# Passage between two stages: one group's chain, two groups' turnings and some unread TensorE products in another order

## The chip, the cores and the metric

The kernel runs on one core of a Trainium2 chip. The core has five engines that run their own instruction lists side by side and wait for each other through semaphores: TensorE (PE), VectorE (DVE), ScalarE (ACT), GpSimd (POOL) and SyncE (SP, which only starts transfers here). The metric is the device time of one launch in microseconds, lower is better.

## The reference

The input `x` is 16 graphs of 512 nodes with 128 channels, `adj` 16 matrices of 512 x 512. The reference adds four blocks to `x`, each on a layer norm of it:

```
x = x + L0_gnn(layernorm(x), adj)      # normalized adjacency times a linear layer, relu
x = x + L0_ffn(layernorm(x))           # one linear layer
x = x + L1_gnn(layernorm(x), adj)      # two convolutions (the second of 17 taps), edge weights exp(-dist),
                                       # messages, a GRU-like update with gates r, z and candidate n
x = x + L1_ffn(layernorm(x))           # 30 steps of the recurrence below

def step(h):                           # h: 16 x 512 x 128
    h = h + 0.01 * tanh(h)
    h = h * sigmoid(h)                 # silu
    h = layernorm(h) * w + bias
    h = h @ W.T + b
```

## The kernel before

**Two stages.** The first stage walks over the 16 graphs; `step(b, p, c, d)` does the last part (gates and update) of graph `b` beside the first parts of the graphs after it. The second stage is the recurrence. Its 64 tiles of 128 tokens are cut into 8 groups of 8 tiles (128 x 1024 values each), and `slot(it, k)` is iteration `it` of group `k` on every engine. Groups depend on nothing but themselves, so all engines work on different groups at one time.

**One group's chain in one iteration.** ACT takes the tanh (`tanh`, L1026), DVE adds 0.01 of it (`scaled_sum`, L1360, tile `u_ring`), ACT takes the silu (`silu`, L1016, tile `g_pair`), DVE takes the statistics of it (`statistics`, L1343), POOL subtracts the mean (`centre`, L525, or `centre_one`, L531), the factor 1/sqrt of the variance comes from POOL (`power`, L516) for groups 0 to 3 of iteration 0 and from a chain of small DVE steps (`root_link`) elsewhere, POOL multiplies (`scale`, L543, tile `h_ring`), PE turns the eight tiles (L959), ACT copies them out (`state`, L1030), and PE multiplies them by the weights of the next iteration (`product_group`, L907) on top of a row of biases (`bias`, L924), which is written between the two halves of a turning.

**Semaphores.** `f_tanh`, `f_u`, `f_silu`, `f_bn`, `f_v`, `f_pow`, `f_norm`, `f_turn`, `f_state`, `f_mm` count these steps in the order of the groups: `f_norm` at 3 means that group 2 is scaled. `bias` for the product of group k waits until the sum of the group that used its banks before is done (`bias_free`, on `f_u`).

**The passage.** The last group (7) needs the last graph's update. In the last two steps of the first stage, `step(15, ...)` and `step(16, ...)` (marked `ends(b, B - 1)` and `ends(b, B)`), groups 0 to 6 of iteration 0 are therefore run in between the work on the last graph: the gates (`gates`, L1494 and L1498), the candidate (L1056), the update (`upd`, L1504, L1507, L1510), its turning on PE (L826), its addition to `x_tok` (L1543), its layer norm (`stats`, `rstd` on POOL, L505 and L507, `last_shift`, L1327, and `last_norm` on ACT, L1049), and then the tanh of group 7. The order of these pieces on every engine is written out by hand, and an engine never runs past a piece that waits. `keep_awake` (L637) issues products of the identity with itself that nobody reads.

**PSUM.** The turning of group j writes two of the banks 4 to 6 (`g_ps`), which the first stage uses as `CONV`, `CHAN` and `DIST_A`; its first half goes into the outer bank, the second into the one shared by even and odd groups.

## Time and profile before

| | us |
|---|---|
| median of 3 runs | 1262.13 (1261.93 to 1262.24) |
| the profiled execution | 1262.43 |
| its span in the trace | 1260.7 |
| PE busy | 1227.7 (97%) |
| DVE busy | 1151.1 (91%) |
| ACT busy | 961.3 (76%) |
| POOL busy | 950.1 (75%) |

The trace's times count from the start of the span. The first stage ends at about 542 us, the recurrence runs alone from about 560 us to the end. "Granted clock" is the share of its full speed that PE's clock was given: 1.00 is 2.4 GHz, 0.50 is 1.2 GHz. A bracket at a row's end is the time the engine sat idle before it and what ended that. Lengths of PE rows overlap, since products are pipelined: the distance from one start to the next is the better measure.

### The profile page before, as it was taken

The page shows a single profiled execution, that of the slowest core. Times are in us where ns is not written, and L with a number is a line of the kernel's source. Part 1 is how long each engine was busy: PE and PEld are TensorE (multiplying, and loading weights), DVE is VectorE, ACT ScalarE, POOL GpSimd, SP SyncE. Part 2 cuts the span into 40 slices and gives each one's busy share as a digit, 9 for nine tenths or more (in the row PEclk, how much of TensorE's full clock was granted, in tenths as well). Part 3 has the DMA queues.
Part 4 walks back from the last instruction along what each step waited for, and adds up shares of the span by engine and source line. Part 5 has one row for each costly group of instructions (what it writes and reads, how often), then busy time and mean ns, then how long its engine had stood idle before and what let it go on. Part 6 is the DMA issues. An engine that isn't in the chain of part 4 may idle for free.

```text
span 1260.7 us, 27945 instructions
## 1 busy us (share of the span) xinstructions
PE 1227.7 (97%) x9073; PEld 1094.8 (87%) x9073; DVE 1151.1 (91%) x3026; ACT 961.3 (76%) x1174; POOL 950.1 (75%) x668
## 2 busy tenths in 40 slices
PE   7899999999999999879999999999999999999998
PEld 6677777777777777669999999999999999999998
DVE  7988888888888887799999999999999999999996
ACT  2455555555555555779999999999999999999994
POOL 2455555555555555589999999999999999999996
PEclk9999999999999999979999999999999999999999
DMA  6111111111111100000000000000000000000004
GB/s 197 43 43 42 43 42 42 42 42 42 42 42 42 41 0 1 1 1 1 1 0 0 0 0 0 0 0 0 0 0 0 0 0 0 0 0 0 0 0 134
DMA packets 29814, 27.78 MB, mean 22 GB/s; under 512 B 3286, under 2 KB 21465, under 8 KB 29657
## 3 DMA queue, kind: packets, MB, share of 16 engines
q1 hardware_dynamic: 29784, 27.41, 6.9%
q8 instruction: 16, 0.26, 0.1%
q14 instruction: 14, 0.11, 0.0%
HBM read 23.21 MB, written 4.19 MB: 22 GB/s over the span
## 4 chain that ended last, share of the span: by engine, by line
PE 47%; DVE 3%; issue 2%; POOL 2%; ACT 1%; DVEq 0%; POOLq 0%
PE psum L907 28%; PE psum L959 15%; PE psum L924 3%; POOL h_ring L543 2%; DVE u_ring L1360 1%; ACT t_ring L1026 1%; DVE f_share L1397 1%; DVE f_stat L1343 1%; DVE psum L1402 0%; DVE psum L1413 0%; DVE psum L1416 0%; DVE f_rs L1431 0%; DVEq L389 0%; DVE y_all L1365 0%; DVEq L1341 0%
## 5 line engine op out<-in xcount | busy, mean ns | idle before, releaser
L543 POOL TENSOR_TENSOR h_ring<-g_pair,f_rs 128x1024 f32<-128x1024 f32 x240 | 452.4, 1906 | 31.2 <-DVE f_rs L1431 18.6
L1343 DVE BATCH_NORM_STATS2 f_stat<-g_pair 128x6 f32<-128x256 f32 x960 | 396.1, 427 | 2.4 <-ACT g_pair L1016 2.4
L959 PE MATMUL psum<-ident,h_ring 128*128 128x128 f32 (+1 forms) x1920 | 297.2, 277 | 4.1 <-POOL h_ring L543 3.1
L1360 DVE SCALAR_TENSOR_TENSOR u_ring<-t_ring,psum 128x1024 f32<-128x1024 f32 x232 | 282.3, 1217 | 5.7 <-issue 2.3
L959 PEld LDWEIGHTS psum<-ident,h_ring 128*128 128x128 f32 (+1 forms) x1920 | 248.1, 167 | 31.4 <-issue 3.7
L907 PE MATMUL psum<-w1c_t,y_all 128*128 128x128 f32 x1920 | 254.7, 276 | 0.0
L1030 ACT ACTIVATE y_all<-psum 128x1024 f32<-128x1024 f32 x240 | 243.9, 1016 | 14.1 <-PE psum L959 14.1
L907 PE MATMUL psum<-w_t,y_all 128*128 128x128 f32 x1920 | 254.5, 276 | 0.0
L1016 ACT ACTIVATE g_pair<-u_ring 128x1024 f32<-128x1024 f32 x240 | 251.7, 1049 | 0.0
L1026 ACT ACTIVATE t_ring<-psum 128x1024 f32<-128x1024 f32 x232 | 238.0, 1026 | 16.2 <-PE psum L907 9.6
L907 PEld LDWEIGHTS psum<-w1c_t,y_all 128*128 128x128 f32 x1920 | 234.6, 193 | 0.0
L907 PEld LDWEIGHTS psum<-w_t,y_all 128*128 128x128 f32 x1920 | 234.3, 192 | 0.0
L525 POOL TENSOR_TENSOR g_pair<-g_pair,f_stat 128x1024 f32<-128x1024 f32 x119 | 227.2, 1909 | 0.0
L505 POOL TENSOR_SCALAR ln_ve<-ln_stat 128x4 f32<-128x4 f32 x64 | 19.4, 302 | 130.7 <-DVE ln_stat L1289 130.7
L1012 ACT ACTIVATE work<-psum 128x512 f32<-128x512 f32 x64 | 34.8, 595 | 96.7 <-PE psum L774 96.6
L924 PE MATMUL psum<-bias,ones_bf 65*128 65x512 bf16 x240 | 92.0, 383 | 0.0
L692 PE MATMUL psum<-diff_s_h,wt_h 128*128 128x256 f32 x272 | 81.8, 301 | 0.0
L694 PE MATMUL psum<-diff_s_h,wt_l 128*128 128x256 f32 x272 | 77.0, 283 | 0.0
L693 PE MATMUL psum<-diff_s_l,wt_h 128*128 128x256 f32 x272 | 76.7, 282 | 0.0
L507 POOL TENSOR_TENSOR ln_rs<-ln_ve,half_neg 128x4 f32<-128x4 f32 x64 | 71.7, 1120 | 5.3
L511 POOL TENSOR_TENSOR work<-work 128x512 f32<-128x512 f32 x32 | 47.0, 1470 | 32.7 <-ACT work L1012 21.0
L1397 DVE TENSOR_REDUCE f_share<-psum 128x16 f32<-128x48 f32 x354 | 68.6, 194 | 0.1
(203 smaller groups left out, 2148.2 us busy)
## 6 DMA issues: line engine op xcount, KB each, us to landing
work<-in_adj_dram SPq DMA_DIRECT2D x16, 1024.0 KB, 5.5
x_tok<-in_x_dram SPq DMA_DIRECT2D x16, 256.0 KB, 5.6
out_dram<-y_all SPq DMA_DIRECT2D x7, 512.0 KB, 3.2
work<-in_L_gnn_conv_w_dram SPq DMA_DIRECT2D x1, 1088.0 KB
out_dram<-y_all SPq DMA_DIRECT2D x2, 256.0 KB, 3.6
work<-in_L_gnn_w_ih_dram SPq DMA_DIRECT2D x1, 384.0 KB
work<-in_L_gnn_w_hh_dram SPq DMA_DIRECT2D x1, 192.0 KB
work<-in_L_gnn_W_dram SPq DMA_DIRECT2D x1, 64.0 KB, 5.4
```

The costliest lines, as they stand in the source:

```text
L525: pool.tensor_tensor(two, two, means, ALU.subtract).then_inc(f_mean, 1)
L543: pool.tensor_tensor(tiles(h_ring[j % 4]), tiles(g_ring[j]), spread(f_rs[:, both(j), at:at + GT], GT, C), ALU.mult).then_inc(f_norm, 1)
L692: pe.matmul(dst, lhs[0], rhs[0], start=start, stop=False)
L907: m = pe.matmul(y_ps[k % 2][:, h, C * t:C * t + C], y_all[:, GT * k + NT * h + t, :], w1c_t[:] if h == centred(k) else w1_t[:], start=(h = ...
L924: pe.matmul(y_ps[k % 2][:, 1 - centred(k), :].rearrange("p (o n) -> p o n", o=2), ones_bf[:], four, start=True, stop=False, skip_group_che ...
L959: m = pe.transpose(g_ps[j % 2][0:rows, t // NT, P * (t % NT):P * (t % NT) + P], tiles(h_ring[j % 4])[:, t, 0:rows], ident[:])
L1016: act.activation(g_ring[j], u_ring[j % 2], ACT.Silu).then_inc(f_silu, 1)
L1026: act.activation(t_ring[k % 2], src, ACT.Tanh).then_inc(f_tanh, 1)
L1030: act.activation(y_all[:, GT * j:GT * j + GT, :].rearrange("p t c -> p (t c)"), g_ps[j % 2].rearrange("p h n -> p (h n)"), ACT.Copy).then_ ...
L1343: ins = dve.bn_stats(f_stat[:, j, 0, 2 * q:2 * q + 2, :].rearrange("p t w -> p (t w)"), two)
L1360: dve.scalar_tensor_tensor(out=u_ring[k % 2], in0=t_ring[k % 2], scalar=STEP, in1=src, op0=ALU.mult, op1=ALU.add).then_inc(f_u, 1)
L1397: dve.tensor_reduce(f_share[:], rows, AX_X, ALU.mult).then_inc(f_link, 1)
```

## The change

The chain of group 2 moves ahead: on ACT its silu stands ahead of the tanh of group 3, on DVE its statistics and variance ahead of the sum of group 3, and on POOL its scaling ahead of the last graph's `rstd`. The turnings of groups 0 and 1 move from the first two slots of PE's recurrence to a place ahead of the turning of the last update, with their copies on ACT (`state`) moved ahead as well. PE gets 12 unread products of 128 x 128 between the two turnings and 8 more (127 rows) ahead of the turning of group 3.

```diff
--- before.py
+++ after.py
@@ -592,10 +592,10 @@
                 if ends(b, B):
                     power(2)
                     centre_one(2)
+                    scale(0, 2, 2)
                 if later(b) and not ends(b, B - 1):
                     rstd(3, b - 1)
                 if ends(b, B):
-                    scale(0, 2, 2)
                     centre_one(3)
                     power(3)
                 if l1:
@@ -631,10 +631,10 @@
         @block.tensor
         def _(pe):
 
-            def keep_awake(bk, count):
+            def keep_awake(bk, count, rows=P):
 
                 for _ in range(count):
-                    pe.matmul(bank[bk][:, 0:P], ident[:], ident[:], start=True, stop=True)
+                    pe.matmul(bank[bk][0:rows, 0:P], ident[:, 0:rows], ident[:], start=True, stop=True)
 
             pe.wait_ge(s_ident, 1)
             keep_awake(DIST_B, 20)
@@ -723,6 +723,36 @@
                     m = pe.transpose(bk[:, P * t:P * t + P], adj_in[p][:, t, P * mt:P * mt + P], ident[:])
                 m.then_inc(s_adj_turned, 1)
 
+            def ones_row(b):
+
+                for t in range(0, NT, 2):
+                    pe.matmul(bank[b][:, C * t:C * t + 2 * C], ones_bf[:],
+                              bias1[:, 2:4, :].rearrange("p t c -> p (t c)"), start=(t == 0), stop=True,
+                              skip_group_check=True)
+
+            def turn_tile(j, n):
+                t = (n + NT * centred(j)) % GT
+                rows = P - 1 if n < NT else P
+                return pe.transpose(g_ps[j % 2][0:rows, t // NT, P * (t % NT):P * (t % NT) + P],
+                                    tiles(h_ring[j % 4])[:, t, 0:rows], ident[:])
+
+            def first_turn(j):
+
+                if j == 0:
+                    pe.wait_ge(s_conv_pre, B)
+                    ones_row(CONV)
+                else:
+                    pe.wait_ge(s_r, B)
+                    ones_row(DIST_A)
+                pe.wait_ge(f_norm, j + 1)
+                for n in range(GT):
+                    if n == NT and j == 0:
+                        pe.wait_ge(s_x_nmp_lo, B)
+                    elif n == NT:
+                        pe.wait_ge(f_state, 1)
+                    m = turn_tile(j, n)
+                m.then_inc(f_turn, 1)
+
             def step(b, p, c, d):
                 q = 1 - p
                 l1 = exists(b)
@@ -819,6 +849,11 @@
 
                     if l1:
                         pe.wait_ge(s_common_read, b + 1)
+                    if ends(b, B):
+                        first_turn(0)
+                        pe.wait_ge(s_msg_pre, B)
+                        keep_awake(TOK, 12)
+                        first_turn(1)
                     pe.wait_ge(s_upd, b)
                     if not l1:
                         pe.wait_ge(s_x3, b - 1)
@@ -924,13 +959,6 @@
                 pe.matmul(y_ps[k % 2][:, 1 - centred(k), :].rearrange("p (o n) -> p o n", o=2), ones_bf[:], four,
                           start=True, stop=False, skip_group_check=True)
 
-            def ones_row(b):
-
-                for t in range(0, NT, 2):
-                    pe.matmul(bank[b][:, C * t:C * t + 2 * C], ones_bf[:],
-                              bias1[:, 2:4, :].rearrange("p t c -> p (t c)"), start=(t == 0), stop=True,
-                              skip_group_check=True)
-
             def slot(it, k):
                 if not ends(it, 0):
                     product_group(it, k)
@@ -938,33 +966,24 @@
                 ahead = not (ends(it, 0) and k < GROUPS - 1) and not (ends(it, ITERS) and k == GROUPS - 1)
                 if before is not None:
                     i, j, s = before
-                    if ends(i, 0) and j == 0:
-                        pe.wait_ge(s_conv_pre, B)
-                        ones_row(CONV)
-                    elif ends(i, 0) and j == 1:
-                        pe.wait_ge(s_r, B)
-                        ones_row(DIST_A)
-                    else:
-                        pe.wait_ge(f_state, s - 1)
+                    pe.wait_ge(f_state, s - 1)
+                    if ends(i, 0) and j == 3:
+                        keep_awake(CHAN + 1, 8, P - 1)
                     pe.wait_ge(f_norm, s + 1)
                 for n in range(GT):
                     if before is not None:
                         if n == NT:
-                            if ends(i, 0) and j == 0:
-                                pe.wait_ge(s_x_nmp_lo, B)
-                            else:
-                                pe.wait_ge(f_state, s)
-                        t = (n + NT * centred(j)) % GT
-                        rows = P - 1 if n < NT else P
-                        m = pe.transpose(g_ps[j % 2][0:rows, t // NT, P * (t % NT):P * (t % NT) + P],
-                                         tiles(h_ring[j % 4])[:, t, 0:rows], ident[:])
+                            pe.wait_ge(f_state, s)
+                        m = turn_tile(j, n)
                     if ahead and n == NT - 1:
                         bias_free(it, k)
                         bias((k + 1) % GROUPS)
                 if before is not None:
                     m.then_inc(f_turn, 1)
 
-            slots(pe, slot, LAG_T, 2)
+            bias_free(0, GROUPS - 1)
+            bias(0)
+            slots(pe, slot, GROUPS, 2)
 
 
 
@@ -1086,13 +1105,13 @@
                     wait(act, s_ffn, c)
                     act.activation(xh_t[:], bank[TURN_B], ACT.Copy).then_inc(s_xt[0], 1)
                 if ends(b, B):
+                    state(0, 0)
                     tanh(0, 4)
                     silu(3, 3)
                     tanh(0, 5)
-                    state(0, 0)
+                    state(1, 1)
                     silu(4, 4)
                     tanh(0, 6)
-                    state(1, 1)
                     silu(5, 5)
                     last_norm()
                 if l1:
@@ -1135,6 +1154,7 @@
                     act.wait_ge(s_nmp, b + 1)
                     act.activation(x_nmp[0][:], bank[CHAN], ACT.Copy).then_inc(s_x_nmp, 1)
                 if ends(b, B - 1):
+                    silu(2, 2)
                     tanh(0, 3)
                 if d is not None:
                     adjt_even(d, p, 2)
@@ -1146,8 +1166,6 @@
                 if ends(b, B - 2):
                     tanh(0, 0)
                     tanh(0, 1)
-                if ends(b, B - 1):
-                    silu(2, 2)
                 if l0:
 
                     act.wait_ge(s_turn[2], c + 1)
@@ -1510,7 +1528,6 @@
                     dve.scalar_tensor_tensor(out=upd[:], in0=upd[:], scalar=0.5, in1=n_act[:],
                                              op0=ALU.mult, op1=ALU.add).then_inc(s_upd, 1)
                 if ends(b, B):
-                    variance(2)
                     scaled_sum(0, 4)
                 if l1:
 
@@ -1605,8 +1622,9 @@
                 if ends(b, B - 1):
                     variance(0)
                     variance(1)
+                    statistics(2, 2)
+                    variance(2)
                     scaled_sum(0, 3)
-                    statistics(2, 2)
                 if l0:
 
                     dve.wait_ge(s_xt[2], c + 1)
```

ACT in the passage, before. `g_pair<-u_ring` is a silu, `t_ring<-y_all` a tanh, `y_all<-psum` a `state`, the three `gates` are gh_n, r and z, `n_act` the candidate.

```order
L1026 ACTIVATE t_ring<-y_all 128x1024
L1145 ACTIVATE gates<-psum,bcol 128x512
L1016 ACT_TABLE_LOAD
L1016 ACTIVATE g_pair<-u_ring 128x1024
L1163 ACTIVATE gates<-psum,bcol 128x512
L1167 ACTIVATE gates<-psum,bcol 128x512
L1056 ACTIVATE n_act<-gates,bcol 128x512
L1026 ACTIVATE t_ring<-y_all 128x1024
L1016 ACTIVATE g_pair<-u_ring 128x1024
L1026 ACTIVATE t_ring<-y_all 128x1024
L1030 ACTIVATE y_all<-psum 128x1024
L1016 ACTIVATE g_pair<-u_ring 128x1024
```

And after the change:

```order
L1035 ACT_TABLE_LOAD
L1035 ACTIVATE g_pair<-u_ring 128x1024
L1045 ACTIVATE t_ring<-y_all 128x1024
L1165 ACTIVATE gates<-psum,bcol 128x512
L1181 ACTIVATE gates<-psum,bcol 128x512
L1185 ACTIVATE gates<-psum,bcol 128x512
L1075 ACTIVATE n_act<-gates,bcol 128x512
L1049 ACTIVATE y_all<-psum 128x1024
L1045 ACTIVATE t_ring<-y_all 128x1024
L1035 ACTIVATE g_pair<-u_ring 128x1024
L1045 ACTIVATE t_ring<-y_all 128x1024
L1049 ACTIVATE y_all<-psum 128x1024
```

The table load and the silu of group 2 have moved ahead of a tanh and gh_n; the first `state` has moved ahead of two tanhs and a silu, the second ahead of the silu of group 4.

POOL in the same place, before. `f_rs` is `power`, L531 `centre_one`, `ln_ve` and `ln_rs` the last graph's `rstd`, `h_ring` `scale`.

```order
L516 TENSOR_TENSOR f_rs<-f_var,half_neg 128x8
L531 TENSOR_TENSOR g_pair<-g_pair,f_stat 128x512
L505 TENSOR_SCALAR ln_ve<-ln_stat 128x4
L507 TENSOR_TENSOR ln_rs<-ln_ve,half_neg 128x4
L543 TENSOR_TENSOR h_ring<-g_pair,f_rs 128x1024
L531 TENSOR_TENSOR g_pair<-g_pair,f_stat 128x512
L516 TENSOR_TENSOR f_rs<-f_var,half_neg 128x8
L543 TENSOR_TENSOR h_ring<-g_pair,f_rs 128x1024
```

After:

```order
L516 TENSOR_TENSOR f_rs<-f_var,half_neg 128x8
L531 TENSOR_TENSOR g_pair<-g_pair,f_stat 128x512
L543 TENSOR_TENSOR h_ring<-g_pair,f_rs 128x1024
L505 TENSOR_SCALAR ln_ve<-ln_stat 128x4
L507 TENSOR_TENSOR ln_rs<-ln_ve,half_neg 128x4
L531 TENSOR_TENSOR g_pair<-g_pair,f_stat 128x512
L516 TENSOR_TENSOR f_rs<-f_var,half_neg 128x8
L543 TENSOR_TENSOR h_ring<-g_pair,f_rs 128x1024
```

The scaling of group 2 has moved ahead of `rstd`; everything else keeps its place.

PE, before, from the last product of the first stage on. `bias` in a row is the row of biases (two of 256 are written ahead of the first turnings).

```order
L694 MATMUL psum<-x_nmp_h,wt_l 128x512
L826 MATMUL psum<-ident,upd 128x128 x4
L930 MATMUL psum<-bias,ones_bf 128x256 x2
L959 MATMUL psum<-ident,h_ring 127x128 x4
L959 MATMUL psum<-ident,h_ring 128x128 x4
L930 MATMUL psum<-bias,ones_bf 128x256 x2
L959 MATMUL psum<-ident,h_ring 127x128 x4
L924 MATMUL psum<-bias,ones_bf 128x512
L959 MATMUL psum<-ident,h_ring 128x128 x4
L907 MATMUL psum<-w1c_t,y_all 128x128 x4
L907 MATMUL psum<-w_t,y_all 128x128 x4
L959 MATMUL psum<-ident,h_ring 127x128 x4
```

After:

```order
L694 MATMUL psum<-x_nmp_h,wt_l 128x512
L729 MATMUL psum<-bias,ones_bf 128x256 x2
L736 MATMUL psum<-ident,h_ring 127x128 x4
L736 MATMUL psum<-ident,h_ring 128x128 x4
L637 MATMUL psum<-ident 128x128 x12
L729 MATMUL psum<-bias,ones_bf 128x256 x2
L736 MATMUL psum<-ident,h_ring 127x128 x4
L736 MATMUL psum<-ident,h_ring 128x128 x4
L861 MATMUL psum<-ident,upd 128x128 x4
L959 MATMUL psum<-bias,ones_bf 128x512
L942 MATMUL psum<-w1c_t,y_all 128x128 x4
L942 MATMUL psum<-w_t,y_all 128x128 x4
```

The turnings of groups 0 and 1 and 12 unread products now stand ahead of the turning of `upd`, which was the first of them. The bias row of group 0's product (128x512), which lay inside the second turning, now stands behind it. Eight more unread products follow further down, between the product of group 1 and the turning of group 3.

On DVE the diff tells it all: the statistics and the variance of group 2 stand ahead of the sum of group 3, which itself stands ahead of everything of `step(16, ...)`.

## Rows read from the trace of the kernel before

**Rows 1.** Part 1 of the page: busy time of each engine.

```profile
PE 1227.7 (97%) x9073; PEld 1094.8 (87%) x9073; DVE 1151.1 (91%) x3026; ACT 961.3 (76%) x1174; POOL 950.1 (75%) x668
```

**Rows 2.** Stretches of the span; columns: from:to, length, busy per engine, granted clock.

```profile
536.00:538.00 2.00, 0.00 (x0) 0.00 (x0) 1.97 (x6) 0.84 (x2) 1.94 (x1) 0.93 0.00 0
546.00:548.00 2.00, 2.00 (x10) 1.70 (x10) 2.00 (x5) 2.00 (x4) 2.00 (x2) 0.51 0.00 0
554.00:556.00 2.00, 0.33 (x1) 0.36 (x2) 2.00 (x9) 2.00 (x3) 2.00 (x2) 0.70 0.00 0
560.00:562.00 2.00, 2.00 (x13) 1.99 (x12) 1.38 (x7) 0.27 (x1) 2.00 (x2) 0.59 0.04 8
560.00:1200.00 640.00, 639.03 (x5446) 614.39 (x5446) 634.43 (x1960) 625.05 (x653) 611.13 (x327) 1.00 0.00 0
```

**Rows 3.** PE in order of time, the passage; columns: start, length, instruction, idle before.

```profile
541.83 1.11 PE L826 MATMUL psum<-ident,upd 128*128 128x128 f32 x4 [6.80 <-DVE upd L1510]
...
550.58 1.06 PE L907 MATMUL psum<-w_t,y_all 128*128 128x128 f32 x8
551.47 1.06 PE L907 MATMUL psum<-w1c_t,y_all 128*128 128x128 f32 x8
555.67 1.19 PE L959 MATMUL psum<-ident,h_ring 128*127 128x128 f32 x4 [3.15 <-POOL h_ring L543]
...
557.22 1.06 PE L959 MATMUL psum<-ident,h_ring 128*128 128x128 f32 x4
558.07 1.91 PE L907 MATMUL psum<-w1c_t,y_all 128*128 128x128 f32 x8
...
562.66 1.06 PE L907 MATMUL psum<-w_t,y_all 128*128 128x128 f32 x8
```

**Rows 4.** ACT in order of time, same stretch and columns.

```profile
529.30 1.05 ACT L1026 ACTIVATE t_ring<-y_all 128x1024 f32<-128x1024 f32 x1
...
531.59 1.28 ACT L1016 ACT_TABLE_LOAD   x1
...
549.79 1.64 ACT L1049 ACTIVATE y_all<-x_tok,ln_shift,ln_rs 128x128 f32<-128x128 f32 x4
...
555.22 1.01 ACT L1030 ACTIVATE y_all<-psum 128x1024 f32<-128x1024 f32 x1
```

**Rows 5.** DVE in order of time, same stretch and columns.

```profile
538.79 2.27 DVE L1507 SCALAR_TENSOR_TENSOR upd<-gates,upd 128x512 f32<-128x512 f32 x1
541.09 0.69 DVE L1510 SCALAR_TENSOR_TENSOR upd<-upd,n_act 128x512 f32<-128x512 f32 x1
...
542.99 0.69 DVE L1543 TENSOR_TENSOR x_tok<-x_tok,psum 128x512 f32<-128x512 f32 x1
...
548.52 0.51 DVE L1327 SCALAR_TENSOR_TENSOR ln_shift<-ln_stat,ln_rs 128x4 f32<-128x4 f32 x1
...
555.55 1.21 DVE L1360 SCALAR_TENSOR_TENSOR u_ring<-t_ring,psum 128x1024 f32<-128x1024 f32 x1
```

**Rows 6.** POOL in order of time, same stretch and columns.

```profile
531.90 1.92 POOL L525 TENSOR_TENSOR g_pair<-g_pair,f_stat 128x1024 f32<-128x1024 f32 x1
533.96 1.90 POOL L543 TENSOR_TENSOR h_ring<-g_pair,f_rs 128x1024 f32<-128x1024 f32 x1
...
538.01 2.49 POOL L543 TENSOR_TENSOR h_ring<-g_pair,f_rs 128x1024 f32<-128x1024 f32 x1
541.94 2.55 POOL L516 TENSOR_TENSOR f_rs<-f_var,half_neg 128x8 f32<-128x8 f32 x1 [1.44 <-DVE f_var L1384]
544.47 1.04 POOL L531 TENSOR_TENSOR g_pair<-g_pair,f_stat 128x512 f32<-128x512 f32 x1
...
546.73 2.28 POOL L543 TENSOR_TENSOR h_ring<-g_pair,f_rs 128x1024 f32<-128x1024 f32 x1
...
551.03 1.64 POOL L516 TENSOR_TENSOR f_rs<-f_var,half_neg 128x8 f32<-128x8 f32 x1
552.75 2.78 POOL L543 TENSOR_TENSOR h_ring<-g_pair,f_rs 128x1024 f32<-128x1024 f32 x1
```

## Prediction

> **What bounds the kernel now.** First the page: PE is busy 97% of the span, DVE 91% [rows 1]. The stretches then say where this share comes from: from 560 us on PE is busy 639.03 of 640 us at full clock [rows 2]. From its re-entry on, the recurrence is PE's own work and nothing is waited for long. The diff touches nothing inside that loop, so the change can only shift the moment at which PE enters it for good. All that follows is read between 528 and 563 us.
>
> PE in order of time shows this passage [rows 3]. After the last gate product it is idle 6.80 us, from 535.0, until DVE's update lets it turn `upd` at 541.83. It works until about 552.4 us, is idle 3.15 us and starts again at 555.67 with the turning of group 3, because `h_ring` of that group is late. From there on no gap follows. The granted clock goes with the idle time [rows 2]: 536 to 538 has a mean of 0.93, so it fell to 1.2 GHz at about 537.7, and it was back at 2.4 GHz by 548.1 (the stretch up to 548 is still 0.51). The second stretch at 1.2 GHz begins at about 554.8 (mean 0.70 from 554 to 556) and ends at about 561.6 (0.59 from 560 to 562). So there is idle time, twice, and half speed, twice; only what delays the entry counts. Between 555.67 and 561.6 PE works at half speed, which costs (561.6 - 555.67) / 2 = 3.0 us.
>
> Two chains end at this entry. On POOL: eight large operations of which each follows the one before it. The first part of the turning of group 3 needs the last of them, the scaling that begins at 552.75 and takes 2.78 [rows 6]. On ACT: `last_norm` begins at 549.79, then come four large operations and the `state` of group 2 at 555.22, which ends at 556.23 [rows 4]. PE's next product of group 2, at 558.07, needs that `state`. Between the halves of the turning stands a bias row, and it waits for the sum of group 0's iteration 1, which DVE ends at 555.55 + 1.21 = 556.76 [rows 5]; the second half starts at 557.22. That sum comes out of the same ACT chain. So even a `h_ring` of group 3 that is there at 553 lets PE do only four turnings; then it stands again until some 7.0 us after `last_norm` begins (556.76 - 549.79).
>
> **The change, part by part.**
>
> ACT: the table load and silu 2 ahead of tanh 3. Both now stand where tanh 3 started, at 529.30 [rows 4]. Load 1.28, silu 1.05 as the tanh: the silu ends at about 531.7 instead of 531.59 + 2.33 = 533.9, 2.2 us earlier. Nothing is added, there is one load as before. Tanh 3 ends at 532.7 instead of 530.35; gh_n follows it, still ahead of gate r.
>
> DVE: statistics and variance of group 2 run 531.8 to 533.2, ahead of the sum of group 3. That sum, which had run beside POOL's `power`, now meets POOL's centring of group 0 (531.90 + 1.92 = 533.82) and scaling of group 0 (from 533.96) [rows 6]. The row that prices this is `upd` at 538.79: 2.27 us against 0.69 for the same kind of operation at 541.09 [rows 5]; it ended 0.56 after POOL's scaling (538.01 + 2.49 = 540.50), as if it had only begun when POOL was through. The Trainium skill ("SBUF — State Buffer", Who interferes with whom) says that a DVE instruction with two SBUF inputs and a GpSimd instruction that reads SBUF exclude each other for a whole instruction; this row agrees. So I lay them one behind the other: sum 3 at 533.8 to 534.9, the scaling of group 0 from 534.9 to 536.8 (before: 535.86), 0.9 us late; if DVE's next gate operation gets in ahead too, 1.5 us late. Bounds: 0 to 1.6. I take 0.9 to 1.5.
>
> POOL after that: `power` 1 and the scaling of group 1 keep their work and end at about 541.2 (between 540.9 and 541.5; before 540.50). Now comes the gain. `power` 2 had waited 1.44 us for its variance and then took 2.55 [rows 6]; the variance has long been there. It runs 1.64, as the row at 551.03, until about 543.2, 544.2 at worst, `centre_one` 1.04 more [rows 6], and the scaling of group 2, ahead of `rstd`, ends at 546.2 to 547.1. Before it ended at 546.73 + 2.28 = 549.01, so 2 to 3 us are won for group 2. PE has no use for them that counts: the turning of group 2 was over at 550.6 and PE idle from 552.4. The last graph's `rstd` pays: it stands behind a scaling of 1.9 us and ends at 547.9 to 549.3 instead of ahead of 546.73, where the scaling began. Then `centre_one`, `power` 3 and the scaling of group 3: 1.04 + 1.64 + 1.9 = 4.6 us and up to 2 us of waiting for DVE's sums, so `h_ring` of group 3 at 552.9 to 555.6 instead of 555.53.
>
> PE: turnings 0 and 1 and the unread products ahead of `upd`. Turning 0 needs `h_ring` 0, at 536.8 to 537.4, and takes 0.9 at full speed. Each unread product is two passes; eight passes take 551.47 - 550.58 = 0.89 us at full speed [rows 3], so 24 take 2.7, and 5.3 at half speed. They run beside the wait for `h_ring` 1 (541.2): at full speed they are hidden and end at 541.1. But PE was idle from 535.0 to 536.8 here and the clock fell at 537.7 before; if it falls again they end at 542.8 or so. Turning 1 then ends at 542.1 or 543.9, and only behind it stands the turning of `upd`, which itself is ready at 539.5 to 543.0. `upd` is turned by 542.9 to 544.4 (before 542.9), and its addition to `x_tok` starts at 543.1 to 544.5 (before 542.99 [rows 5]). On ACT the two early `state` copies cost 1.0 each, as the one at 555.22; what hides them is that ACT, with all before silu 5 done by 547, waits for DVE's sum of group 5 in any case.
>
> What the addition decides: behind it DVE has statistics 0.9, the statistics of group 3 1.4, the sum of group 5 1.2, the statistics of group 4 1.4 and `last_shift`, together 5.6 us from its start: 548.6 before, plus a wait (`last_shift` took 0.51 us from 548.52 [rows 5]). `last_norm` could thus have begun at 549.0 (548.52 + 0.51); it began at 549.79, since ACT was still busy. ACT is free earlier now, so this bound falls away, and DVE's takes its place: 543.1 to 544.5 plus 5.6 plus up to 0.8 of waiting for POOL gives 548.7 to 550.9. The middle is 550.0, 0.2 us later than before. The second half of turning 3 starts at 550.0 + 7.4 = 557.4 instead of 557.22, and group 2's product at 558.3.
>
> The 8 unread products ahead of turning 3: 1.8 us at full speed behind the product of group 1, which ends at 550.2 to 552. They end at 552 to 553.8 and are hidden, as PE waits until 557.4 in any case, but for four turnings. From 553.8 at the latest, and 554.4 with those, 3 us or more of nearly nothing remain; a gap of 3.15 us lowered the clock before. So I expect the second stretch at 1.2 GHz again, with the same end near 561.6 and the same cost.
>
> Sum: profiled execution 1262.43 + 0.2 = 1262.6. The median of the runs is 0.30 below the profiled one, so 1262.3 us. My forecast for itself spans 1261.6 to 1263.3.
>
> **Rivals.** Times are for the median. A difference of under 0.2% (2.5 us) is what a measurement of this kernel can't tell from none.
>
> A. The clock stays up. If the unread products and the four early turnings of group 3 keep it at 2.4 GHz, PE does the work from 557.2 on at full speed: 0.4 for the second half, 1.8 for the product, 559.5. Then it needs `h_ring` 4, which POOL can't end before 559.3 to 559.7, and 1.1 for turning it: 560.6 instead of 562.66 [rows 3], 2.1 us won. With `last_norm` at 549.0 it is 2.8. For it: the first idle stretch of 6.8 us is filled. Against it: the wait in front of the bias is not filled. 1260.0, a chance of 0.2.
>
> B. The queue in front of `upd` (the side of slower). Mechanism: the clock falls at 537.7, the 24 passes run at half speed, turning 1 and `upd` come late, `x_tok` at 545.1 instead of 542.99. It decides once the addition starts after 544.2; each 1 us from there is 1 us at the entry: 0.9 us. PE then enters so late, or with a stop in front of the bias, that the clock comes back later: the first stretch at 1.2 GHz lasted 10.4 us against 6.8 of the second [rows 2], half of the difference is 1.8. Together 2.7: 1264.8. The late `upd` alone has a chance of 0.3 and is worth under 1; with the clock 0.13.
>
> C. The change does not do what it says: `h_ring` 2 not earlier, because DVE's sums take the place of POOL's old wait. Then `rstd`, behind a scaling that ends at 549.01 as before, would end at 550.3 (1.3 us more, as from 545.5 to the scaling's start at 546.73), `last_norm` would begin at 550.8, 1.0 late, and the time would be 1263.1. The chance is 0.1.
>
> **How the numbers follow.** Forecast (0 to +1 around) 0.57, A 0.2, B with the clock 0.13, C 0.1. Of A about two thirds reach 2.5 us, of B nearly all, of C and the forecast nearly nothing: faster by over 0.2% 0.13, slower 0.13, within it 0.74. The range from 1260.1 to 1264.5 leaves out half of A and most of B, less than 0.2.
>
> **What would show it.** In the profile after: silu 2 ending near 531.7; no idle time of POOL near 541; `h_ring` 2 at 546.2 to 547.1 and `h_ring` 3 by 555.6; PE rows of `upd` at 542.5 to 544; `last_norm` between 549 and 551; PE's second half of turning 3 some 7.4 us behind it; clock at half from 555 to 561.6. I am wrong if PE stays at 2.4 GHz through 555 to 561, if `last_norm` moves by over 1 us, or if the stretch from 563 us to the end changes its length.

## The result and the profile after

The changed kernel takes 1264.28 us (median of 22 runs, 1263.07 to 1265.48) against 1261.91 us (22 runs, 1260.85 to 1262.96) of the kernel before: ratio 1.0018, 95% interval 1.0012 to 1.0024. It is 2.4 us slower, 0.18%. The time was forecast at 1262.3 in a range of 1260.1 to 1264.5; the side was right, the size of the loss was not.

The profiled execution has a span of 1262.8 us. The loop did not change: from the product of group 3 (562.66 before [rows 3], 564.74 after) to the last product row of each trace (1254.92 and 1256.98) they take 692.3 and 692.2 us. Of the 2.1 us between the two traces, 0.24 are there at the sum of group 2 (527.74 before, 527.98 after), before the first moved instruction, and fall to no part of the change: the trace after has a short stretch at 1.2 GHz near its start (0.93 from 10 to 15 us, 0.73 from 15 to 20) that the trace before lacks. The other 1.8 us arise in the passage.

The profile after, PE in order of time (start, length, instruction, idle time before it). L736 is a turning, L637 the unread products, L861 the turning of `upd`, L959 the bias row, L942 a product.

```profile
536.94 1.14 PE L736 MATMUL psum<-ident,h_ring 128*127 128x128 f32 x8 [1.44 <-POOL h_ring L543]
537.92 2.84 PE L637 MATMUL psum<-ident 128*128 128x128 f32 x24
...
542.87 0.66 PE L861 MATMUL psum<-ident,upd 128*128 128x128 f32 x4
...
554.71 0.71 PE L736 MATMUL psum<-ident,h_ring 128*127 128x128 f32 x4 [2.78 <-POOL h_ring L543]
558.78 0.61 PE L959 MATMUL psum<-bias,ones_bf 65*128 65x512 bf16 x1 [3.36 <-DVE u_ring L1378]
559.18 1.06 PE L736 MATMUL psum<-ident,h_ring 128*128 128x128 f32 x4
...
564.74 1.06 PE L942 MATMUL psum<-w_t,y_all 128*128 128x128 f32 x8
```

These answer to [rows 3]. The first idle stretch (6.80 us) is filled but for waits of 1.44, 0.61 and 1.08 us, and the clock stayed up through it. The first half of turning 3 comes at 554.71, counted from the sum of group 2 (the start of the passage) 1.2 us earlier than before. But then PE stands 3.36 us ahead of the bias row, which had followed at once before, and the second half comes at 559.18 instead of 557.22.

ACT, DVE and POOL after, in three parts, the same columns. L1068 is `last_norm`, L1345 `last_shift`, L1378 the sums, L543 the scalings, L507 the end of `rstd`, L516 `power`.

```profile
530.96 1.06 ACT L1035 ACTIVATE g_pair<-u_ring 128x1024 f32<-128x1024 f32 x1
...
550.08 1.65 ACT L1068 ACTIVATE y_all<-x_tok,ln_shift,ln_rs 128x128 f32<-128x128 f32 x4 [0.84 <-DVE ln_shift L1345]
...
555.77 1.06 ACT L1035 ACTIVATE g_pair<-u_ring 128x1024 f32<-128x1024 f32 x1 [1.10 <-DVE u_ring L1378]
```

```profile
535.05 2.38 DVE L1512 SCALAR_TENSOR_TENSOR gates<-gates 128x512 f32<-128x512 f32 x1
...
543.87 0.68 DVE L1560 TENSOR_TENSOR x_tok<-x_tok,psum 128x512 f32<-128x512 f32 x1
...
549.42 0.63 DVE L1345 SCALAR_TENSOR_TENSOR ln_shift<-ln_stat,ln_rs 128x4 f32<-128x4 f32 x1
...
552.85 2.89 DVE L1378 SCALAR_TENSOR_TENSOR u_ring<-t_ring,y_all 128x1024 f32<-128x1024 f32 x1 [0.33 <-ACT t_ring L1045]
...
557.52 1.20 DVE L1378 SCALAR_TENSOR_TENSOR u_ring<-t_ring,psum 128x1024 f32<-128x1024 f32 x1
```

```profile
534.20 2.69 POOL L543 TENSOR_TENSOR h_ring<-g_pair,f_rs 128x1024 f32<-128x1024 f32 x1
...
541.50 2.09 POOL L516 TENSOR_TENSOR f_rs<-f_var,half_neg 128x8 f32<-128x8 f32 x1
...
545.00 1.90 POOL L543 TENSOR_TENSOR h_ring<-g_pair,f_rs 128x1024 f32<-128x1024 f32 x1
...
547.14 1.87 POOL L507 TENSOR_TENSOR ln_rs<-ln_ve,half_neg 128x4 f32<-128x4 f32 x1
548.99 1.04 POOL L531 TENSOR_TENSOR g_pair<-g_pair,f_stat 128x512 f32<-128x512 f32 x1
549.99 2.69 POOL L516 TENSOR_TENSOR f_rs<-f_var,half_neg 128x8 f32<-128x8 f32 x1
552.76 1.90 POOL L543 TENSOR_TENSOR h_ring<-g_pair,f_rs 128x1024 f32<-128x1024 f32 x1
```

The row to look for is DVE's at 552.85: the sum of group 7 takes 2.89 us. Before, it began at 552.55 and took 1.23:

```profile
552.55 1.23 DVE L1360 SCALAR_TENSOR_TENSOR u_ring<-t_ring,y_all 128x1024 f32<-128x1024 f32 x1 [1.04 <-ACT t_ring L1026]
```

POOL's scaling of group 3, from 552.75, took 2.78 [rows 6] instead of 1.90. The sum begins 0.09 us behind POOL where it had been 0.20 us ahead. Which of the two moved is read from the start of the passage, the sum of group 2, since the whole passage lies 0.24 us later in this trace. Counted from there the sum of group 7 comes 0.06 us later (24.81 and 24.87), with `last_norm` (22.05 and 22.10), and POOL's scaling comes 0.23 us earlier (25.01 and 24.78). So the order turned mainly because POOL was early. DVE now waits for POOL where POOL had waited for DVE. POOL's 0.9 us had cost nothing; DVE's 1.7 us lie on the chain to the bias row, and ACT's silu of group 7 waits for it too (1.10 us idle).

The granted clock after, in stretches (from:to, length, busy times, clock):

```profile
538.00:540.00 2.00, 2.00 (x20) 2.00 (x20) 1.97 (x7) 1.81 (x3) 1.92 (x2) 1.00 0.00 0
556.00:558.00 2.00, 0.00 (x0) 0.00 (x0) 2.00 (x9) 2.00 (x3) 1.51 (x1) 0.75 0.00 0
562.00:564.00 2.00, 2.00 (x12) 2.00 (x12) 1.34 (x7) 0.31 (x1) 2.00 (x2) 0.54 0.00 0
```

In the passage there is one stretch at 1.2 GHz left, from about 557 to 563.8, and it lies over PE's re-entry as the second one did before [rows 2].

### The profile page after: what moved, and what is told of

It reads as the page before. It is cut to its first block, busy times and chain, and to the rows that moved or that the text cites. A ratio compares the mean times of both kernels' runs of the same rounds, so it can differ in the third digit from the quotient of the medians.

```text
span 1262.8 us, 28024 instructions
## 1 busy us (share of the span) xinstructions
PE 1232.4 (98%) x9113; PEld 1098.6 (87%) x9113; DVE 1153.8 (91%) x3026; ACT 961.7 (76%) x1174; POOL 951.3 (75%) x668
## 4 chain that ended last, share of the span: by engine, by line
PE 77%; DVE 11%; issue 4%; ACT 3%; POOL 2%; DVEq 0%; DMA 0%; SPq 0%; POOLq 0%; ACTq 0%
PE psum L942 28%; PE psum L736 15%; PE psum L692 5%; PE psum L694 5%; PE psum L693 5%; PE psum L898 4%; PE psum L959 3%; PE psum L714 3%; PE psum L709 3%; POOL h_ring L543 2%; DVE u_ring L1378 1%; PE psum L723 1%; PE psum L703 1%; DVE emb_n L1556 1%; ACT t_ring L1045 1%
## 5 line engine op out<-in xcount | busy, mean ns | idle before, releaser
L543 POOL TENSOR_TENSOR h_ring<-g_pair,f_rs 128x1024 f32<-128x1024 f32 x240 | 451.9, 1904 | 33.2 <-DVE f_rs L1449 20.6
L736 PE MATMUL psum<-ident,h_ring 128*128 128x128 f32 (+1 forms) x1920 | 295.2, 276 | 6.1 <-POOL h_ring L543 5.1
L1378 DVE SCALAR_TENSOR_TENSOR u_ring<-t_ring,psum 128x1024 f32<-128x1024 f32 x232 | 281.7, 1214 | 6.0 <-issue 2.3
L736 PEld LDWEIGHTS psum<-ident,h_ring 128*128 128x128 f32 (+1 forms) x1920 | 246.0, 166 | 33.8 <-POOL h_ring L543 9.0
L942 PE MATMUL psum<-w_t,y_all 128*128 128x128 f32 x1920 | 254.5, 276 | 0.0
L942 PE MATMUL psum<-w1c_t,y_all 128*128 128x128 f32 x1920 | 254.5, 276 | 0.0
L942 PEld LDWEIGHTS psum<-w_t,y_all 128*128 128x128 f32 x1920 | 234.3, 192 | 0.0
L942 PEld LDWEIGHTS psum<-w1c_t,y_all 128*128 128x128 f32 x1920 | 234.3, 192 | 0.0
L959 PE MATMUL psum<-bias,ones_bf 65*128 65x512 bf16 x240 | 91.8, 382 | 4.4 <-DVE u_ring L1378 3.4
L507 POOL TENSOR_TENSOR ln_rs<-ln_ve,half_neg 128x4 f32<-128x4 f32 x64 | 72.5, 1133 | 5.3
```

Of the source, the lines that this page charges most:

```text
L543: pool.tensor_tensor(tiles(h_ring[j % 4]), tiles(g_ring[j]), spread(f_rs[:, both(j), at:at + GT], GT, C), ALU.mult).then_inc(f_norm, 1)
L736: return pe.transpose(g_ps[j % 2][0:rows, t // NT, P * (t % NT):P * (t % NT) + P], tiles(h_ring[j % 4])[:, t, 0:rows], ident[:])
L942: m = pe.matmul(y_ps[k % 2][:, h, C * t:C * t + C], y_all[:, GT * k + NT * h + t, :], w1c_t[:] if h == centred(k) else w1_t[:], start=(h = ...
L1378: dve.scalar_tensor_tensor(out=u_ring[k % 2], in0=t_ring[k % 2], scalar=STEP, in1=src, op0=ALU.mult, op1=ALU.add).then_inc(f_u, 1)
```

## The experiments

Each was timed beside the kernel before on the same chip (11 runs each, e2 7). The expectations weigh three explanations of the loss. "Port order" is my theory: a sum of DVE and an operation of POOL exclude each other, the one that begins first goes on and the other waits for its end, and at the sum of group 7 this order has turned. "Queue in front of upd" is rival B of the prediction, and "clock" is a half-speed stretch that ends later for reasons of its own.

The sum of group 2 is the last large instruction ahead of all that was moved, and it starts between 527.02 and 528.14 us in the ten traces; so distances are compared, not times. Five of them carry the readings: from the sum of group 2 to `last_norm` (a), from `last_norm` to the sum of group 0 in iteration 1 that frees the bias row (b), the length of the sum of group 7, from the sum of group 2 to the bias row of turning 3 (bias), and from there to the first product of group 3 (c), behind which PE is in the loop. The sum of the last two says when PE enters it: 34.92 us before, 36.76 after the change.

| kernel | median us | ratio to before (95% interval) | a | b | sum 7 | bias | c |
|---|---|---|---|---|---|---|---|
| before | 1261.9 | 1 | 22.05 | 5.76 | 1.23 | 29.08 | 5.84 |
| changed | 1264.28 | 1.0018 (1.0012 to 1.0024) | 22.10 | 7.44 | 2.89 | 30.80 | 5.96 |
| e1_hold | 1261.55 | 0.9997 (0.9988 to 1.0006) | 22.09 | 5.77 | 1.22 | 29.16 | 4.78 |
| e2_before_late | 1266.04 | 1.0032 (1.0020 to 1.0043) | 22.06 | 9.58 | 2.81 | 32.91 | 6.03 |
| e3_turns_only | 1259.87 | 0.9985 (0.9976 to 0.9994) | 21.26 | 5.77 | 1.23 | 29.19 | 3.55 |
| e4_chain_only | 1263.49 | 1.0015 (1.0006 to 1.0024) | 22.84 | 6.85 | 2.30 | 30.95 | 4.91 |
| e5_no_unread | 1262.52 | 1.0006 (0.9997 to 1.0015) | 22.30 | 5.91 | 1.35 | 29.47 | 5.72 |
| e6_hold_28 | 1260.76 | 0.9992 (0.9983 to 1.0001) | 22.10 | 5.79 | 1.23 | 29.16 | 4.22 |
| e7_turns_filled | 1259.74 | 0.9983 (0.9974 to 0.9992) | 21.27 | 5.79 | 1.23 | 28.70 | 3.82 |
| e8_pool_undone | 1260.73 | 0.9991 (0.9982 to 1.0000) | 21.96 | 5.78 | 1.23 | 29.01 | 4.20 |

The columns split what happens at the entry. The change loses 1.72 us up to the bias row and 0.12 behind it. The kernels that are faster than before (e3, e6, e7, e8) write the bias row at nearly the same distance as before, 28.70 to 29.19 us against 29.08; what they win lies nearly all behind it, in c, where PE turns and multiplies at 2.4 GHz instead of 1.2.

**e1_hold**, the changed kernel with the meeting of the two taken away:

```diff
 def scale(i, j, s):
     ...
+    if ends(i, 0) and j == 3:
+        pool.wait_ge(f_u, 8)
     at = GT * (j % 2)
```

> The changed kernel, and POOL waits ahead of the scaling of group 3 until DVE's sum of group 7 is done (f_u at 8); nothing else differs. Port order (my theory): in the changed kernel that sum took 2.89 us instead of 1.2, since POOL's scaling of group 3 began 0.09 us before it. With the wait the sum takes 1.2 us, the scaling starts near 554.0 and h_ring of group 3 comes at 556, which is still ahead of the bias row; the bias row of turning 3 comes at 557.1 instead of 558.78, and the time falls by 1.7 us to 1262.6. Queue in front of upd (rival): the loss comes from x_tok, late by 0.6 us, and all behind it; the wait changes nothing there and the scaling comes 1.3 us later: 1264.3 or up to 1.3 more. Clock (rival): the second stretch at 1.2 GHz ended at 563.6 instead of 561.6 of itself; the time stays at 1264.3.

Measured: 1261.55 us, 2.7 less than the changed kernel. The sum takes 1.22 us again, POOL idles 1.56 us, its scaling comes 1.5 us later (26.26 behind the sum of group 2 instead of 24.78), and b is back at 5.77. The first two blocks are DVE and POOL of this kernel, the third PE.

```profile
552.05 1.22 DVE L1380 SCALAR_TENSOR_TENSOR u_ring<-t_ring,y_all 128x1024 f32<-128x1024 f32 x1 [0.33 <-ACT t_ring L1047]
```

```profile
549.19 2.69 POOL L516 TENSOR_TENSOR f_rs<-f_var,half_neg 128x8 f32<-128x8 f32 x1
553.45 1.90 POOL L545 TENSOR_TENSOR h_ring<-g_pair,f_rs 128x1024 f32<-128x1024 f32 x1 [1.56 <-DVE u_ring L1380]
```

```profile
555.40 1.16 PE L738 MATMUL psum<-ident,h_ring 128*127 128x128 f32 x4 [4.26 <-POOL h_ring L545]
556.35 0.63 PE L961 MATMUL psum<-bias,ones_bf 65*128 65x512 bf16 x1
556.78 1.06 PE L738 MATMUL psum<-ident,h_ring 128*128 128x128 f32 x4
...
561.13 1.06 PE L944 MATMUL psum<-w_t,y_all 128*128 128x128 f32 x8
```

A wait more makes the changed kernel faster. This is the port order's outcome and neither rival's. It is 1.0 us more than the 1.7 that the sum explains. The traces say where the two parts lie: the bias row comes 1.64 us earlier, as expected, and 1.18 us more are won behind it (c 4.78 instead of 5.96), since the half-speed stretch was short here (clock 0.87 from 554 to 556, 0.50 from 556 to 558 and 0.77 from 558 to 560). The other runs agree: the mean granted clock of all 11 is 0.9975, that of the changed kernel's 22 is 0.9958.

**e2_before_late**, the kernel before with the order of the changed one forced on it:

```diff
 def scaled_sum(it, k):
     ...
     wait(dve, f_silu, s - 1)
+    if ends(it, 0) and k == 7:
+        dve.wait_ge(f_norm, 4)
```

> The kernel before, and DVE waits ahead of the sum of group 7 until POOL has scaled group 3 (f_norm at 4): the order that the changed kernel falls into, forced on the old one. Port order: POOL's scaling runs 552.75 to 554.65 (1.9 instead of 2.78), the sum ends at 555.9 instead of 553.78, the bias row of turning 3 comes 2.1 us later, and the time rises by 2.1 us to 1264.0. Queue in front of upd: this kernel has no such queue, and h_ring of group 3 comes 0.9 us earlier: 1261.9 or less. Clock: 1261.9.

Measured: 1266.04 us, 4.2 more than before, with nothing of the change in it but the order of two instructions, which a wait forces. That is twice what I had expected. DVE and POOL of this kernel show why:

```profile
554.56 2.81 DVE L1362 SCALAR_TENSOR_TENSOR u_ring<-t_ring,y_all 128x1024 f32<-128x1024 f32 x1 [3.26 <-POOL h_ring L543]
```

```profile
552.53 1.90 POOL L543 TENSOR_TENSOR h_ring<-g_pair,f_rs 128x1024 f32<-128x1024 f32 x1
554.38 1.91 POOL L525 TENSOR_TENSOR g_pair<-g_pair,f_stat 128x1024 f32<-128x1024 f32 x1
```

The sum, let go when the scaling ends, meets POOL's next instruction at once and waits for that one as well: b grows by 3.8 us. So e2 shows the direction and more than the size of what the changed kernel lost, where the sum waited for one instruction only. The scaling of group 3 takes 1.90 us here, and `h_ring` comes earlier than in the kernel before, which is of no use.

**e3_turns_only** leaves of the change only the early turnings of groups 0 and 1, their `state` copies and the unread products:

```diff
 # POOL, step(16): scale(0, 2, 2) behind rstd(3, ...) again
 # ACT, step(15): silu(2, 2) behind tanh(0, 3) and gh_n again
 # DVE: scaled_sum(0, 3) ahead of statistics(2, 2); variance(2) behind the update again
```

> The changed kernel with group 2's chain put back on ACT, DVE and POOL; only the early turnings with their copies and the unread products are left of the change. Port order: POOL and DVE meet as in the kernel before, the sum of group 7 comes first; ACT is free for last_norm, which starts 0.7 us earlier, at 549.1: 1261.2. Queue in front of upd: the turning of upd comes behind 24 passes and a turning, x_tok at 543.5 to 544 instead of 542.99: 1262.4 to 1264.3.

Measured: 1259.87 us, 2.0 less than before, 4.4 less than the change. `last_norm` comes 0.8 us earlier (a), as expected, and x_tok's addition is not late: it starts 15.17 us behind the sum of group 2, and 15.25 before. The sum of group 7 begins 0.91 us ahead of POOL's scaling and is clear of it. The early turnings with the unread products are thus a gain, and the queue in front of `upd` is no cost here.

The gain does not come by way of the earlier `last_norm`, though. PE of this kernel:

```profile
552.97 1.82 PE L942 MATMUL psum<-w1c_t,y_all 128*128 128x128 f32 x8
554.63 1.94 PE L637 MATMUL psum<-ident 128*127 128x128 f32 x16
556.40 0.61 PE L736 MATMUL psum<-ident,h_ring 128*127 128x128 f32 x4
556.84 0.38 PE L959 MATMUL psum<-bias,ones_bf 65*128 65x512 bf16 x1
...
560.39 1.06 PE L942 MATMUL psum<-w_t,y_all 128*128 128x128 f32 x8
```

The sum that frees the bias row ended at 555.90, but PE was still at its own work, the first part of it at 1.2 GHz, and wrote the row 29.19 us behind the sum of group 2, 0.1 us later than before. What is won is c, 3.55 us instead of 5.84: the half-speed stretch lay ahead of the re-entry (clock 0.50 from 548 to 554) and not over it.

**e4_chain_only** is the other half: the kernel before with the moves of group 2's chain on POOL, ACT and DVE, and PE's order left.

> The kernel before with only group 2's chain moved ahead on ACT, DVE and POOL; PE's order and the state copies stay. Port order: upd is late by 1.0 us (DVE and POOL exclude each other around 534 to 537), ACT's chain with it, so last_norm starts at 550.8; the scaling of group 3 starts ahead of the sum of group 7, which loses another 1 us or so: 1263.9. Queue in front of upd: there is none here, and the time is 1261.9 to 1262.9.

Measured: 1263.49 us, 1.6 more than before. `last_norm` is 0.8 us later, the sum of group 7 begins 0.68 us behind POOL's scaling and takes 2.30. Both losses are of the expected kind and size; the bias row comes 1.87 us later, and in this trace 0.93 of that come back in c. DVE's row, then POOL's:

```profile
552.62 2.30 DVE L1359 SCALAR_TENSOR_TENSOR u_ring<-t_ring,y_all 128x1024 f32<-128x1024 f32 x1 [0.91 <-ACT t_ring L1026]
```

```profile
551.94 1.90 POOL L543 TENSOR_TENSOR h_ring<-g_pair,f_rs 128x1024 f32<-128x1024 f32 x1
```

**e5_no_unread** drops both `keep_awake` calls from the changed kernel.

> The changed kernel without its 12 and 8 unread products. Port order (my theory): they run beside waits and lie on no path; upd, x_tok, last_norm and the sum of group 7 come at the same times, and turning 3 is already at half speed with them: 1264.3, at most 1 us more where the clock falls more often. Queue in front of upd (rival): 24 passes leave the queue ahead of the turning of upd, x_tok comes earlier by up to 0.6 us: 1263.7 or less.

Measured: 1262.52 us, 1.8 less. Neither expectation holds. x_tok's addition came not earlier but later (16.59 us behind the sum of group 2, 15.89 in the changed kernel), for the clock fell: 0.50 from 542 to 544. By this delay the sum of group 5 came at 19.66 us behind the sum of group 2 instead of 18.95, while the last graph's `rstd` began at 19.2 in both. So `rstd` ran in 1.01 us ahead of that sum, where in the changed kernel it took 1.87 us behind it. POOL's `power` 3 began 0.46 us ahead of the sum of group 6 and took 1.64 instead of 2.69, and the scaling of group 3 began 1.62 us ahead of the sum of group 7, which lost only 0.1 us by it (1.35):

```profile
546.33 1.01 POOL L507 TENSOR_TENSOR ln_rs<-ln_ve,half_neg 128x4 f32<-128x4 f32 x1
547.30 1.63 POOL L531 TENSOR_TENSOR g_pair<-g_pair,f_stat 128x512 f32<-128x512 f32 x1
548.89 1.64 POOL L516 TENSOR_TENSOR f_rs<-f_var,half_neg 128x8 f32<-128x8 f32 x1
550.61 1.90 POOL L543 TENSOR_TENSOR h_ring<-g_pair,f_rs 128x1024 f32<-128x1024 f32 x1
```

So in these two traces the unread products cost nothing by lying in the queue; they placed DVE and POOL so that they met, and without them the bias row comes 1.33 us earlier. The theory held, but I had taken the meeting for granted instead of working out whether it would still take place.

**e8_pool_undone** puts back one line, POOL's scaling of group 2 behind `rstd`; PE, ACT and DVE are those of the changed kernel.

> The changed kernel with only POOL's order put back: rstd of the last graph ahead of the scaling of group 2 again. rstd ends near 546.9 instead of 549.0, last_norm comes at 549.6 instead of 550.1, the tanh of group 7 ends at 552.3, POOL's scaling of group 3 starts at about 552 to 553.5. Port order: the time depends on which of the two comes first; if the sum does, it takes 1.2 us and the bias row comes at 556.5: 1262.0; if not, 1263.8. Queue in front of upd: that queue is unchanged and x_tok as late as in the changed kernel: 1264.3.

Measured: 1260.73 us, 3.5 less than the changed kernel and 1.1 less than before. The sum comes first (551.79, 1.23 us) and POOL's scaling behind it (552.70, 2.07). This line alone decides about the loss: without it the rest of the change is at the edge of a gain (the interval ends at 1.0000). I had expected 1262.0 for this case with the bias row at 556.5 on the changed kernel's clock. It came at 556.07 in a trace that runs 0.92 us ahead of that one, so 0.5 us later than expected. The time was lower than expected all the same, because PE was at full speed by then: c is 4.20 us instead of 5.96, which is half of the 3.5 us. The bias row gives the other half (29.01 instead of 30.80).

**e6_hold_28 and e7_turns_filled** ask for the clock's share. The first is e1 with 28 unread products instead of 8, the second e3 with

```diff
                 pe.wait_ge(f_state, s - 1)
+                if ends(i, 0) and j == 2:
+                    keep_awake(CONV, 14, P - 1)
                 if ends(i, 0) and j == 3:
-                    keep_awake(CHAN + 1, 8, P - 1)
+                    keep_awake(CHAN + 1, 18, P - 1)
```

> The changed kernel with the wait of the first experiment (sum of group 7 first) and 28 unread products ahead of turning 3 in place of 8. The 8 ended at 551.1 there and PE stood 4.3 us; 28 take 6.2 us and end at 555.4, as h_ring of group 3 comes. If the half clock at the entry still costs time, PE now turns and multiplies at full speed from 555.4 on, until h_ring of group 4 (559.2) bounds it: 0.8 us less than without, 1260.8. If the entry is bounded by the bias row and h_ring of group 4 alone, 1261.5. If the 28 products run at half speed themselves they end at 561 and the time is over 1264.

> The third experiment (early turnings only, group 2's chain as before the change) with 14 unread products ahead of turning 2 and 18 instead of 8 ahead of turning 3. There the clock fell at 548.3, PE having stood 3.3 us ahead of turning 2, and product and turnings up to 555.1 ran at half speed. Filled, it stays at 2.4 GHz; the bias row of turning 3 comes right behind the sum at 555.9 instead of 556.84, the next product at 556.8 instead of 557.5; h_ring of group 4 at 558.8 then bounds PE: 0.5 us less, 1259.4. If the clock is no part of it: 1259.9. If the added products come in the way of turning 2 (h_ring at 548.9): up to 1 us more.

Measured: 1260.76 us, 0.8 less than e1, as expected. PE of e6 stays at full clock (1.00 in every stretch from 540 to 562), and the wait goes to `h_ring` of group 4:

```profile
549.08 6.37 PE L639 MATMUL psum<-ident 128*127 128x128 f32 x56
555.28 0.69 PE L738 MATMUL psum<-ident,h_ring 128*127 128x128 f32 x4
556.21 0.39 PE L961 MATMUL psum<-bias,ones_bf 65*128 65x512 bf16 x1 [0.23 <-DVE u_ring L1380]
...
559.26 0.68 PE L738 MATMUL psum<-ident,h_ring 128*127 128x128 f32 x4 [0.44 <-POOL h_ring L545]
```

The 0.8 us are what the clock still cost in e1, whose half-speed stretch was short. Against the kernel before, with the bias row at the same distance, c is 4.22 us instead of 5.84.

e7 took 1259.74 us against 1259.87 of e3: no difference that these runs can tell, where 0.5 was expected. The bias row comes 0.49 us earlier in its trace, as expected, but 0.27 of that go again in c. In e3's trace the half-speed stretch lay ahead of the re-entry (from about 547.8 to 554.5, and not from 548.3 to 555.1 as my expectation has it), where it costs little. e7 is the fastest kernel of the study, 2.1 us (0.17%, interval 0.08 to 0.26%) under the kernel before and 4.5 under the change; e3, which differs from it by nothing measurable, has the simpler code.

## Why the prediction was right and wrong

**Right: what bounds the passage.** `last_norm` at 550.08 was forecast at 550.0; counted from the sum of group 2 it is 0.05 us later than before, where 0.2 was forecast. Behind it the bias row, not `h_ring` of group 3, lets PE in: `h_ring` came at 554.66, 0.9 us earlier than before on the trace's clock, and bought nothing, as in e2. The loop kept its length. One reading of [rows 6] was loose: of POOL's large operations not each follows the one before it, as `power` 2 had waited 1.44 us for its variance.

**Right: the steps on ACT, DVE and POOL up to 549 us.** Silu 2 ended at 532.0 (531.7 forecast). The scaling of group 0 ended at 536.89 (536.8), DVE's gate operation waited for it (2.38 us), POOL had no idle time near 541, `h_ring` of group 2 ended at 546.90 (546.2 to 547.1), the last graph's `rstd` at 549.01 (547.9 to 549.3). x_tok's addition came at 543.87 (543.1 to 544.5).

**Wrong: "PE's second half of turning 3 some 7.4 us behind" `last_norm`.** It came 9.1 us behind. This is the term that was mis-sized, and it holds nearly all of the 1.8 us that arose in the passage: b grew by 1.68 us. I took the stretch from `last_norm` to the bias row as a constant, since none of its instructions was moved. I had used the exclusion of DVE's and POOL's instructions elsewhere, and for this place too, but only one way round: "up to 2 us of waiting for DVE's sums", POOL's wait. [rows 6] showed a scaling of 2.78 us, which says that the sum had got in just ahead of it; the trace has it at 552.55, 0.20 us ahead. My own forecast moved both against this margin, `last_norm` by 0.2 us and POOL's scaling by up to 2.6 (its end at 552.9 to 555.6 instead of 555.53). e1 and e2 show the cause from both sides: the order of these two instructions, put right in the changed kernel, gives back 2.7 us, of which 1.64 lie ahead of the bias row, and put wrong in the old one it costs 4.2, with a second instruction to wait for.

**What turned the margin** is shown by e8 to be the order on POOL. With `rstd` first, the sum of group 7 comes 0.14 us earlier and POOL's scaling 0.86 us later (25.64 behind the sum of group 2 instead of 24.78), because POOL's scaling of group 2 and centring of group 3 each wait for one of DVE's sums there (2.98 and 2.09 us, in the changed kernel 1.90 and 1.04). Group 2's chain on ACT and DVE makes `last_norm` 0.7 us later (e8 against e3: 21.96 and 21.26) and the time 0.9 (1260.73 and 1259.87, with intervals of the ratios that overlap).

**Rival A, the clock stays up:** half of it took place. The first half-speed stretch is gone from the profile; `last_norm` came no earlier by it, and what it was worth was not isolated. The second stayed, as forecast: PE had stood 2.78 us ahead of turning 3 and stood 3.36 more ahead of the bias row. It is no part of the loss (c 5.84 and 5.96). Its price is large all the same, and the faster kernels live on it: c is 1.6 us shorter than before in e6 and e8, 2.0 in e7 and 2.3 in e3. The 2.1 that I gave it had the right size, and so had the bound by `h_ring` of group 4: PE gets it in e6 at 559.26, which is 559.95 on the clock of the kernel before, where 559.3 to 559.7 was forecast.

**Rival B, the queue in front of `upd`:** wrong as a mechanism. The clock did not fall at 537.7, the 24 passes took 2.84 us, and e3 has the same queue and is the second fastest. The addition to `x_tok` is 0.6 us late in the changed kernel and 0.8 in e4, which has no such queue, and not late in e3, which has it; in e8, where only POOL's order is put back, it is 0.6 late. So the delay comes with group 2's chain on ACT and DVE. The rival's price of 2.7 us came near the measured loss by chance. **Rival C** did not happen: `h_ring` 2 was early.

**Open:** why the clock came back sooner in e1 than in the changed kernel, which is worth the 1.0 us of e1's 2.7 that the sum does not explain, and what decides in general where the half-speed stretch falls. e3 and e8 gained by its place without being built for it. Open too is the difference between the 2.4 us of the medians and the 1.8 that the passage shows in the two traces, as only one execution of each kernel was traced.

## What to carry to other kernels

Where two engines exclude each other on an instruction, look at each such pair near the critical chain and write down which comes first and by how much; a margin of 0.2 us between two instructions of 1.2 and 1.9 us is a term of the sum, even if nothing there is edited. If the order matters, fix it with a wait, as in e1: the engine with slack should be the one that waits. Then split the time at the entry into the part up to the wait that ends last and the part behind it: here the order of two instructions moved the first, and the place of PE's half-speed stretch moved the second by as much, so that a kernel can win for another reason than the one it was written for (e3). And an operation moved ahead pays only if its result is what somebody waits for; here the early scaling of group 2 gave a result that PE had no use for, and by sparing POOL two waits it brought POOL's next scaling ahead of the sum on which the end hung.

## What the runs showed of the hardware that was not expected

An instruction that loses once can lose twice: in e2 the sum was ready at the moment when POOL's scaling ended, POOL's centring began 0.18 us ahead of it, and the sum took 2.81 us. POOL's `power`, an operation of 1.64 us on few values, can lose too: it took 2.69 when one of DVE's sums had begun 0.02 us ahead of it (549.97 and 549.99 in the changed kernel). The other way round neither lost. In the kernel before, `power` began first, and the sum of group 3 ran beside it in its usual length; DVE's row, then POOL's:

```profile
530.39 1.23 DVE L1360 SCALAR_TENSOR_TENSOR u_ring<-t_ring,y_all 128x1024 f32<-128x1024 f32 x1
```

```profile
530.29 1.64 POOL L516 TENSOR_TENSOR f_rs<-f_var,half_neg 128x8 f32<-128x8 f32 x1 [0.20 <-DVE f_var L1384]
```

So the exclusion did not last for the whole of this instruction. The Trainium skill ("SBUF — State Buffer", Who interferes with whom) states that what decides is the order of issue and not the kind of operation. For the sum of group 7 and POOL's scaling the traces of e1 and of the changed kernel agree, with the same two instructions and 1.22 and 2.89 us for the sum.

Place and length of the half-speed stretch at the entry differ from trace to trace: 554.8 to 561.6 before, about 557 to 563.8 after, 555.5 to 558.9 in e1, 547.8 to 554.5 in e3, 550.2 to 553.7 in e8. The runs of one kernel differ with it. The 22 of the kernel before spread over 2.1 us (1260.85 to 1262.96), the 11 of e6 and of e7, whose traces have no such stretch in the passage, over 0.8 (1260.26 to 1261.03) and 1.1 (1259.47 to 1260.58). Of the changed kernel's 22 runs the seven with a mean clock of 0.997 average 1263.5 us, the eleven with 0.994 or 0.995 average 1264.7.
